# Value products of the third and fourth key tile issued one behind the other in causal phases: a hybrid attention and tree-FFN kernel

## What is computed

```
x = x + attn_a(layernorm(x))     # 16 heads of 16 dims, 4096 tokens as 8 elements x 512, no mask
x = x + ffn(layernorm(x))        # 8 levels of sigmoid gates over 256 leaves, leaf_prob @ leaf_values, output matrix
x = x + attn_b(layernorm(x))     # as attn_a, with rotary angles and a causal mask
x = x + ffn(layernorm(x))        # the same network and weights

scores = einsum('bhqd,bhkd->bhqk', q, k) / sqrt(16)
scores = where(causal, scores, -1e9)          # attn_b only
out    = einsum('bhqk,bhkd->bhqd', softmax(scores), v)
```

## Time and profile before

| | us |
|---|---|
| median of three runs | 1144.35 |
| lowest and highest run | 1141.99, 1144.99 |
| the profiled execution | 1141.19 |
| its span in the trace | 1139.5 |
| PE busy (matmuls) | 1075.6, 94% of the span |
| DVE busy | 883.5, 78% |
| ACT busy | 761.6, 67% |
| POOL busy | 307.0, 27% |

### The profile page before, as it was taken

The page is one execution under the profiler, slowest core; times in us unless marked ns, Lnnn a source line. Parts: engine busy times, 40 slices in busy tenths (PEclk is TensorE's granted clock), DMA queues, the critical chain, the costliest instruction groups (busy, mean ns, idle before and its releaser), DMA issues.

```text
span 1139.5 us, 18953 instructions
## 1 busy us (share of the span) xinstructions
PE 1075.6 (94%) x6164; PEld 543.1 (48%) x6164; DVE 883.5 (78%) x2481; ACT 761.6 (67%) x1565; POOL 307.0 (27%) x339
## 2 busy tenths in 40 slices
PE   5899999999999999999999999999999898989986
PEld 3323444444445444554455544454444555545544
DVE  4887787787868897687977878788886878777844
ACT  3577767677776678765777767776776666666562
POOL 3011110114213150222403151131513526262210
PEclk9999999999999999999999999999999999999999
DMA  8150501402205131321305023051311313022001
GB/s 240 49 128 19 130 20 50 99 20 85 83 20 130 38 107 43 99 70 38 111 20 149 20 66 102 19 131 35 103 50 40 110 38 122 28 85 65 20 20 37
DMA packets 79778, 80.97 MB, mean 71 GB/s; under 512 B 13088, under 2 KB 68672, under 8 KB 79680
## 3 DMA queue, kind: packets, MB, share of 16 engines
q1 hardware_dynamic: 79616, 79.73, 24.6%
q0 software_dynamic: 64, 0.03, 0.0%
HBM read 20.71 MB, written 8.39 MB: 26 GB/s over the span
## 4 chain that ended last, share of the span: by engine, by line
PE 59%; DVE 22%; ACT 7%; issue 4%; SPq 3%; POOL 2%; DMA 1%; POOLq 0%; DVEq 0%; ACTq 0%
PE ps_work L1304 13%; PE ps_out L1213 12%; PE ps_max L1167 11%; PE ps_key L1189 11%; DVE neg_max L916 8%; PE ps_work L1343 7%; ACT probs L797 4%; PE ps_work L1269 3%; DVE scratch L1073 3%; DVE ps_max L912 2%; SPq L538 2%; DVE scratch L1103 2%; DVE scratch L1076 2%; ACT turned_block L818 2%; DVE moments L1021 1%
## 5 line engine op out<-in xcount | busy, mean ns | idle before, releaser
L797 ACT ACTIVATE probs<-ps_key 128x512 f32<-128x512 f32 (+3 forms) x1024 | 515.4, 520 | 297.2 <-PE ps_key L1189 291.5
L916 DVE TENSOR_REDUCE neg_max<-ps_max 128x1 bf16<-128x512 f32 x512 | 336.9, 684 | 86.5 <-PE ps_max L1167 85.2
L1167 PE MATMUL ps_max<-k_stack,q_stack 96*128 96x512 bf16 (+3 forms) x1024 | 347.0, 345 | 24.0 <-DVE neg_max L912 10.0
L1189 PE MATMUL ps_key<-q_stack,k_stack 97*128 97x512 bf16 (+3 forms) x1024 | 348.4, 343 | 16.0 <-ACT probs L797 10.5
L912 DVE CUSTOM_DVE_ANT_0 ps_max<-ps_max,mask_b 128x128 f32<-128x128 f32 (+3 forms) x512 | 247.1, 504 | 105.5 <-PE ps_max L1167 102.7
L1213 PE MATMUL ps_out<-probs,v_ones 128*32 128x512 f32 (+3 forms) x2048 | 233.8, 529 | 0.6 <-POOL probs L688 0.6
L1167 PEld LDWEIGHTS ps_max<-k_stack,q_stack 96*128 96x128 bf16 x1024 | 99.4, 97 | 277.1 <-DVE neg_max L916 109.8
L688 POOL TENSOR_SCALAR_AFFINE_SELECT probs<-probs 128x512 f32<-128x512 f32 x128 | 82.2, 643 | 402.3 <-ACT probs L797 401.7
L1189 PEld LDWEIGHTS ps_key<-q_stack,k_stack 97*128 97x128 bf16 x1024 | 100.9, 99 | 139.7 <-ACT probs L797 87.6
L1213 PEld LDWEIGHTS ps_out<-probs,v_ones 128*32 128x32 f32 x2048 | 40.4, 108 | 73.7 <-issue 65.3
L912 DVE DVE_READ_ACCUMULATOR2_ANT neg_max<- 128x1 bf16 x512 | 72.8, 142 | 0.0
(11 more groups left out here) (93 smaller groups left out, 1254.1 us busy)
## 6 DMA issues: line engine op xcount, KB each, us to landing
k_stack<-k_part SPq DMA_DIRECT2D x108, 128.0 KB, 2.4
q_stack<-q_part SPq DMA_DIRECT2D x108, 128.0 KB, 2.4
k_stack<-k_part SPq DMA_DIRECT2D x42, 256.0 KB
q_stack<-q_part SPq DMA_DIRECT2D x42, 256.0 KB
x_in<-in_x SPq DMA_DIRECT2D x8, 512.0 KB, 3.9
q_stack<-shift_rows SPq DMA_DIRECT2D x256, 1.0 KB, 1.7
x_again<-in_x SPq DMA_DIRECT2D x8, 512.0 KB, 3.9
spill<-x_plain SPq DMA_DIRECT2D x8, 512.0 KB, 2.8
```

What stands on the lines that cost most here:

```text
L797: act.activation(probs[step % RING][:, j, q0:T], ps_key[slot % 2][:, 0:T - q0], ACT.Exp, scale=SCALE).then_inc(on["exp_done"], 1)
L916: dve.tensor_reduce(out=dst, in_=src, axis=AX_X, op=ALU.max, negate=True)\
L1167: pe.matmul(dst[:, 0:keys], q_stack[n % 2][0:SPLIT_ROWS, h, P * qt:P * qt + P], k_stack[n % 2][0:SPLIT_ROWS, h, 0:keys], start=True, stop= ...
L1189: pe.matmul(ps_key[slot % 2][:, 0:T - q0], k_stack[n % 2][0:STACK_ROWS, h, P * kb:P * kb + P], q_stack[n % 2][0:STACK_ROWS, h, q0:T], star ...
```

## The change

In a causal phase the value products of key tile 2 no longer stand in their own slot (16 from the start of their group, or slot 0 of the next phase) but four slots later, right in front of those of key tile 3. Plain phases, the other two key tiles, and `closing` stay as they are. The products, their waits (`causal_done` once for each step) and their counts are the same; only their place in the order of PE changes.

```diff
                 by_key(n, slot)
                 if slot % GROUP == MIX_LAG % GROUP:
-                    step = (slot - MIX_LAG) // GROUP
-                    if step >= 0:
-                        mixed(n, step, MIX_LAG - GROUP + 1)
-                    elif n > 0:
-                        mixed(n - 1, step + STEPS, MIX_LAG - GROUP + 1)
+                    m, step = n, (slot - MIX_LAG) // GROUP
+                    if step < 0:
+                        m, step = n - 1, step + STEPS
+
+                    if m >= 0 and not (causal(m) and step % TILES == TILES - 2):
+                        if causal(m) and step % TILES == TILES - 1:
+                            mixed(m, step - 1, MIX_LAG + 1)
+                        mixed(m, step, MIX_LAG - GROUP + 1)
```

## The result

The changed kernel takes 1154.9 us (median of four runs, 1152.82 to 1156.43) against 1143.17 us for the kernel before in the same comparison. The ratio is 1.0094, with a 95% interval of 1.0074 to 1.0113: the change costs 0.7 to 1.1%. The profiled execution took 1155.0 us with a span of 1153.2, 13.7 us more span than before.

The account below looks back on a forecast made before the run. PE was busy 94%, but the chain of waits decided slot by slot. Entered slots 12.4 + 0.6, less 4.7 and 0.05 given back, made +8.2 us on the 1144.35 us median: 1152.5 us, range 1147 to 1157.5 us.

Parts of the forecast that it names:

- the joined group: Where two value-product groups stand together, the added 256 columns cost PE 0.48 us, between bounds of 0.43 and 0.57.
- what the border pairs leave: Seven pairs moving from slot 0 to slot 4 of the next phase give back 0.67 us each, 4.7 us.
- What they leave: Removals at slots 16, 32, 48 give back nothing except 0.05 us in phase 15; seven at slot 0 give 4.7 us.
- What one move is worth on PE: On PE alone, a lone 256-column group costs 0.67 us, a joined one 0.48; each pair saves 0.19 us.
- The entry (0.10 us) and the way out (0.14 us): Constants around a value-product group on PE: 0.09 to 0.10 us ahead of it, 0.14 us left over beyond its columns.
- The second 0.43 us in the sum: The last 128-column group in the chain, at 1.2 GHz: the bare columns of another 256 cost 0.43 us more.
- What they enter: 25 of 31 entered groups are in the chain, adding 12.4 us; three partly hidden at slot 52 add 0.6 us.
- the transfers of the earlier trace: In phases 12 to 14, SyncE transfers, the last ending at 905.79, hold PE up in slot 36 and hide slot 20.
- Rival (a): Time left at slots 16, 32, 48 comes back too: 5.9 us faster, 1138.5 us; chance 0.06.
- Rival (b): Later PE idle, at slots 34 and 49, swallows the longer slots: +4.4 or +2.4 us, 1146.8 us; chance 0.10.
- Rival (d): The two groups do not stand together, PE waiting for tile 3's mask: full drain, +10.9 us; chance 0.04.
- Rival (c): New idle before slot 49 lowers PE's clock, some 2 us each time, up to 8 us in four phases; chance 0.12.

Follow-up runs that it names:

- the border pairs alone: Only the seven pairs leaving slot 0 for slot 4 of the next phase joined, against the kernel before the change: 1139.77 us, ratio 0.9986.
- the kernel with both groups apart: Changed kernel with a score product put between the 256- and 128-column groups, against the kernel before the change: 1162.21 us, ratio 1.0164.
- the extra products: Changed kernel with three overwritten score products added in slot 49 of phases 4, 6, 8, 10, against the kernel before: 1147.35 and 1148.74 us, ratios 1.0057 and 1.0064.

## Why the prediction was right, and where it was off

The forecast was slower, +8.2 us, 1152.5 us, 1147 to 1157.5 us; measured were +10.8 us by the ratio of the first comparison (0.94% of 1143.17) and 1154.9 us. The sign and its reason are shown; three terms were off: the joined group, what the border pairs leave, and the clock.

**What they leave.** Right. The score product of slot 18 keeps its distance of 2.02 us from slot 15; slots 32 and 48 give nothing back either. Behind slot 32 the product of slot 34 comes 0.26 us early, and slot 36 is as late as slot 32 was; behind slot 48 the product of slot 49 comes 0.43 us early, and slot 50 is as late as slot 48 was. The products that the earlier trace rows name are those of slots 35 and 51, not 34 and 49. The views that decided it were the chain of waits at those slots, not the 94% of the earlier trace rows. Of the seven border pairs, the four behind phases 4, 6, 8 and 10 gave back 0.67 us each, as read from the earlier trace rows. The other three gave back 0.53, 0.53 and 0.35 us: the slot was PE's in the chain, but its removal came back only in part; with the border pairs alone PE then waits 0.19 us for a maximum of DVE early in phase 15, where it did not wait before. The term of 4.7 us should have been 4.1 us.

**What one move is worth on PE.** The entry (0.10 us) and the way out (0.14 us) were right, as the kernel with both groups apart shows. The joined group was mis-sized: I took 0.48 us, between 0.43 and 0.57, with two more turns inside; it is 0.43 us, the bare columns, the lower bound. A joined pair lasts 0.79 us, just as one 384-column group does in the kernel before:

```profile
611.67 0.85 PE L1213 MATMUL ps_out<-probs,v_ones 128*32 128x384 f32 x8
612.46 0.28 PE L1167 MATMUL ps_max<-k_stack,q_stack 96*128 96x256 bf16 x1
```

On 25 pairs that is 1.2 us too much in the sum. With this, 0.5 us for slot 52 (below) and the border pairs corrected, the sum is 25 x 0.43 + 0.43 + 0.5 - 4.1 = +7.6 us. The two comparisons of the changed kernel without its falls at slot 49 gave +6.5 and +7.3 us (ratios 1.0057 and 1.0064). The second 0.43 us in the sum, for a low clock at slot 52 of phase 15, came in one of the three profiled executions of the changed kernel; in the other two the clock is up there, where it is low in the kernel before, and the changed kernel gets 0.8 us less late by slot 56.

**What they enter.** Right: 0.43 us for each pair of phases 4 to 10, nothing for slot 20 of phases 12 to 14, and 0.15, 0.15 and 0.23 us for slot 52 there, where I took 0.2. But what hides slot 20 is not first the transfers of the earlier trace rows. PE's wait for a maximum of DVE in slot 24 of phase 12 shortens by the same 0.4 us (the first row is the kernel's before):

```profile
891.96 0.23 PE L1167 MATMUL ps_max<-k_stack,q_stack 96*128 96x128 bf16 x1 [1.08 <-DVE neg_max L912]
900.18 0.23 PE L1167 MATMUL ps_max<-k_stack,q_stack 96*128 96x128 bf16 x1 [0.66 <-DVE neg_max L912]
```

**Rival (a), faster,** fell with the distance of 2.02 us. **Rival (b), swallowed,** fell too: the lateness of slot 24 is still there at slots 32 and 36, and that of slot 40 at slots 48 and 50, through all the idle between. **Rival (d)** fell with the 0.79 us.

**Rival (c), the clock.** The step that failed is its chance. I had the numbers side by side, some 1.7 us of 3.4 left of PE's work against 1.60 and 1.61 us before falls, and still gave it 0.12; in the three profiled executions of the changed kernel it came in ten of twelve phases. Nothing in the rows spoke for so low a chance; that the clock was up there in the kernel before is no reason, since the new idle is just what changes. Its price was over-sized, 2 us for each fall where 1.0 to 1.3 us were measured. By estimate, 3.4 us at half the clock leave 1.7 us of work undone, and 0.4 to 0.7 us of that fell into slack. The three or four falls of an execution make 3.8 to 4.3 us of span.

The corrected +7.6 us and these 3.8 to 4.3 us are +11.4 to +11.9 us. The three comparisons of the changed kernel gave +10.8, +8.5 and +10.4 us, each with an interval of some 2 us either way. The sum lies above all three, and above the end of the second one's interval (+11.1 us), so it accounts for the size only roughly. Of the 13.7 us of the first profiled execution 8.2 us are there at the start of phase 12; 2.7 us come in phase 12, 1.6 us of them by its fall, 0.3 us in phases 13 to 15, and 2.5 us in the closing part. That the median lay as near the forecast as it did is in part luck: 1.2 us too much for the joining stood against 0.6 us too little for the border pairs and nothing for the clock.

Two figures of the prediction do not follow from its own lines. A third of (b) adds 0.03, so the chances of "slower" come to 0.87, not 0.86. And the highest value that its cases give is 1156.7 us (1155.3 + 1.4), where the range ends at 1157.5 us; the measured time lies inside either.

The rule of the Trainium skill that I weighed, in TensorEngine Tiling (Array Packing), Key Properties, that a change of tiling mode drains TensorE, agrees with these traces: 0.24 us for a way in and out, and none between two groups of the same layout. It gives a reason for the saving; the size comes from the rows, and it says nothing of who is waiting.

## What to carry to other kernels

Before work is moved on the busiest engine, look in the chain of waits at the place that it leaves and at the place that it enters; the move gains only what the first gives back, and pays in full at the second. A place is worth no more than the slack of the engine that is late next, so a removal that pays for a short group need not pay for a long one. And an idle stretch of TensorE that gets longer, here by 0.67 us that were free in themselves, can cost 1.0 to 1.3 us in clock behind it; overwritten products in such a stretch are a cheap test of whether it does.

## What the runs showed of the hardware

- Two groups of column-tiled value products in a row, 16 instructions with 16 weight loads, take what their columns take and 0.14 us once. I had expected 0.02 to 0.03 us for each turn between four and four products.
- Whether the clock falls behind the same stretch of the same program changes from phase to phase and from execution to execution: four of four phases in one, three of four in two others, at 1.0 to 1.3 us each. That this widens the spread of the whole kernel is not shown: it is 6.4 us (1149.49 to 1155.84 us in six runs), and 7.3 us (1144.78 to 1152.04 us in six runs) with the extra products, whose profiled executions have no fall there.
- A fall ahead of a wait for transfers can be hidden by it in part or in full. The kernel before has one in slot 24 of phases 12, 13 and 14 each; the changed kernel has none there and is 1.0 to 1.2 us less late in slot 28, but by slot 36, where PE waits for the transfers of the earlier trace rows, all of that is gone in phase 12, and 0.6 and 0.3 us are left in phases 13 and 14.
